# Gated attention block, last stage: GpSimd adds scaled expert outputs in pairs before TensorE sums them

## What is computed

```python
x1 = _layer_norm(x + attn_out, ln1_w, ln1_b)
gates = jax.nn.softmax(x1 @ gate_w.T + gate_b, axis=-1)
_, top_idx = jax.lax.top_k(gates, TOP_K)          # TOP_K = 2 of 8 experts
top_gates = jnp.take_along_axis(gates, top_idx, axis=-1)
expert_outputs = jnp.einsum('bsd,efd->bsef', x1, expert_w) + expert_b[None, None]
sel = jnp.take_along_axis(expert_outputs, top_idx[..., None], axis=2)
moe_out = jnp.sum(sel * top_gates[..., None], axis=2)
return _layer_norm(x1 + moe_out, ln2_w, ln2_b)
```

## Time and profile before

| | us |
|---|---|
| median of 3 runs | 565.8 (564.96 to 565.97) |
| the profiled execution, whole | 566.44 |
| its span, first to last instruction | 564.6 |
| PE busy | 457.0 (81%) |
| DVE busy | 375.2 (66%) |
| POOL busy | 352.3 (62%) |
| ACT busy | 278.5 (49%) |

### The profile page before, as it was taken

One profiled execution on the slowest core, in us unless ns is written; L12 is line 12 of the kernel. 1 busy time (PEld: TensorE's weight loads), 2 busy tenths in 40 slices (PEclk: granted clock), 3 DMA queues, 4 the chain that ended last, 5 costly groups with the idle time before them and its releaser, 6 DMA issues.

```text
span 564.6 us, 16099 instructions
## 1 busy us (share of the span) xinstructions
PE 457.0 (81%) x5728; PEld 281.9 (50%) x5728; DVE 375.2 (66%) x1159; ACT 278.5 (49%) x693; POOL 352.3 (62%) x734
## 2 busy tenths in 40 slices
PE   0247766666667788999999999998969999999993
PEld 0123433333334444666666666664645666666652
DVE  5254665555556757777777777775337899999981
ACT  1114654444444646656566666664644554455431
POOL 3564556553556779988887887851113666766654
PEclk9999977776777869999999999999998999999995
DMA  3344454433444443434344344342000000000000
GB/s 105 94 120 105 105 152 116 110 94 95 110 113 104 103 99 90 98 95 99 96 106 99 96 97 101 95 97 63 9 2 1 10 20 19 20 11 20 20 19 19
DMA packets 96014, 42.72 MB, mean 76 GB/s; under 512 B 19896, under 2 KB 95808, under 8 KB 95936
## 3 DMA queue, kind: packets, MB, share of 16 engines
q1 hardware_dynamic: 86720, 39.60, 27.9%
q10 hardware_dynamic: 9216, 2.10, 1.9%
HBM read 5.75 MB, written 2.10 MB: 14 GB/s over the span
## 4 chain that ended last, share of the span: by engine, by line
SPq 35%; PE 25%; DVE 17%; POOL 12%; issue 6%; DMA 2%; ACT 2%; POOLq 0%; ACTq 0%; DVEq 0%
SPq L192 29%; PE u_bank L426 5%; DVE z_acc L914 4%; PE s_bank L379 3%; PE s_bank L369 3%; POOL xn_all L243 3%; SPq L168 2%; PE u_bank L765 2%; PE s_bank L744 2%; DMA kst<-part 2%; PE st_bank L744 2%; SPq L203 2%; PE u_bank L439 2%; POOL z_rstd_ L642 1%; POOL rstd L233 1%
## 5 line engine op out<-in xcount | busy, mean ns | idle before, releaser
L593 DVE TENSOR_REDUCE nm<-s_bank 128x4 f32<-128x512 f32 x256 | 174.0, 686 | 128.6 <-PE s_bank L379 127.3
L504 ACT ACTIVATE pt<-st_bank 128x512 f32<-128x512 f32 x256 | 150.2, 598 | 144.2 <-PE st_bank L379 105.0
L379 PE MATMUL s_bank<-kst,qst 64*128 64x128 bf16 x1024 | 110.7, 239 | 51.3 <-DMA kst<-part 48.1
L426 PE MATMUL u_bank<-pt,vaug 128*32 128x128 f32 x2048 | 119.2, 309 | 0.1
L379 PEld LDWEIGHTS s_bank<-kst,qst 64*128 64x128 bf16 x1024 | 73.3, 102 | 81.5 <-DMA kst<-part 47.1
L379 PE MATMUL st_bank<-qst,kst 64*128 64x128 bf16 x1024 | 111.2, 235 | 0.0
L379 PEld LDWEIGHTS st_bank<-qst,kst 64*128 64x128 bf16 x1024 | 74.2, 101 | 0.4
L426 PEld LDWEIGHTS u_bank<-pt,vaug 128*32 128x32 f32 x2048 | 42.4, 113 | 31.3 <-issue 8.1
L369 PE MATMUL s_bank<-mqk,esel 64*128 64x256 bf16 x256 | 50.2, 276 | 3.1 <-DMA kst<-part 2.7
L369 PE MATMUL st_bank<-mkq,esel 64*128 64x256 bf16 x256 | 50.2, 276 | 0.0
L285 POOL TENSOR_TENSOR part<-r,part 128x512 bf16<-128x512 f32 x32 | 37.0, 1156 | 2.7
(11 more groups left out here) (118 smaller groups left out, 897.9 us busy)
## 6 DMA issues: line engine op xcount, KB each, us to landing
qst<-part SPq DMA_DIRECT2D x224, 64.0 KB, 2.1
kst<-part SPq DMA_DIRECT2D x224, 64.0 KB, 2.1
x_all<-x SPq DMA_DIRECT2D x16, 128.0 KB, 2.5
c_all<-ctx_in SPq DMA_DIRECT2D x16, 128.0 KB, 2.6
qst<-qrow SPq DMA_DIRECT2D x32, 64.0 KB, 2.1
qst<-mts ACTq DMA_DIRECT2D x64, 32.0 KB, 2.1
out<-z_o SPq DMA_DIRECT2D x16, 128.0 KB, 1.8
ewt<-exp_t SPq DMA_DIRECT2D x1, 512.0 KB
```

The lines of the kernel that those rows point to most:

```text
L379: return pe.matmul(bank[:, j * P:(j + 1) * P], k if keys_first else q, q if keys_first else k, start=not masked, stop=True, skip_group_che ...
L426: ins = pe.matmul(u_bank[b][32 * j:32 * j + 32, r * P:(r + 1) * P], v, pt[m % 4][:, j, :], start=half == 0, stop=half == 1, skip_group_che ...
L504: act.activation(pt[m % 4][:, :, :].rearrange("k j q -> k (j q)"), st_bank[m % 2][:, :], ACT.Exp).then_inc(ex, 1)
L593: dve.tensor_reduce(nm[q % 2][:, first:first + HEADS], s_bank[n % 2][:, :].rearrange("q (j k) -> q j k", j=HEADS), AX_X, ALU.max, negate=T ...
```

## The change

GpSimd adds the four scaled tiles of each sequence two and two (experts 4 and 6, 5 and 7) in one instruction of 128x512 elements, into a new tile `z_gated_pairs`. `gated_sum` then multiplies two tiles by the identity instead of four. A new semaphore `z_yp` stands between them. `gate_experts` now waits for `z_yp` (the pairs of the group before have been added) in place of `z_yb`; the new instruction waits for `z_yg` (ACT has scaled) and, because `z_gated_pairs` is a single buffer, for `z_yb` of the group before. POOL calls the new function last in its step, for group `s - 2`.

```diff
@@ PE, gated_sum
                 pe.wait_ge(z_gtc, g + 1)
-                pe.wait_ge(z_yg, g + 1)
+                pe.wait_ge(z_yp, g + 1)
                 for b in range(G):
                     dst = u_bank[0][:, b * P:(b + 1) * P]
                     pe.matmul(dst, zgt[i][:, b * P:(b + 1) * P], ebs[:, :], start=True, stop=False)
-                    for e in range(HALF):
-                        ins = pe.matmul(dst, idf[:, :], zyg[:, b, e, :], start=False, stop=e == HALF - 1)
+                    for e in range(HALF // 2):
+                        ins = pe.matmul(dst, idf[:, :], zyp[:, b, e, :], start=False, stop=e == HALF // 2 - 1)
                 ins.then_inc(z_yb, 1)
@@ ACT, gate_experts
                 if gc >= 1:
-                    act.wait_ge(z_yb, g)
+                    act.wait_ge(z_yp, g)
@@ POOL
+            def gated_pairs(g, gc):
+                pool.wait_ge(z_yg, g + 1)
+                if gc >= 1:
+                    pool.wait_ge(z_yb, g)
+                pool.tensor_tensor(zyp[:, :, :, :], zyg[:, :, 0:HALF // 2, :], zyg[:, :, HALF // 2:HALF, :],
+                                   ALU.add).then_inc(z_yp, 1)
+
@@ POOL, body
                 if in_z(c, 3):
                     factor2(s - 3, c - 3)
+                if in_z(c, 2):
+                    gated_pairs(s - 2, c - 2)
```

More of the change, by code:

```diff
@@ L659, in gated_block_kernel @@
         zrs2 = sb("z_rstd2_", [P, G]); zy = sb("z_y2", [P, G, P]); zyw = sb("z_yw", [P, G, P])
-        zsum = sb("z_x1_moe", [P, G, P]); zyg = sb("z_gated", [P, G, HALF, P]); zyb = sb("z_ywb", [P, G, P]); zo = two("z_o", [P, G, P])
+        zsum = sb("z_x1_moe", [P, G, P]); zyg = sb("z_gated", [P, G, HALF, P]); zyp = sb("z_gated_pairs", [P, G, HALF // 2, P]); zyb = sb("z_ywb", [P, G, P]); zo = two("z_o", [P, G, P])
         z_at = sem("z_att_copied"); z_ot = sem("z_att_transposed"); z_otc = sem("z_att_t_copied")
@@ L666, in gated_block_kernel @@
         z_gate = sem("z_gate_steps"); z_exp = sem("z_gate_exp"); z_gt = sem("z_gates_transposed")
-        z_gtc = sem("z_gates_t_copied"); z_y = [sem(f"z_experts{k}") for k in range(2)]; z_yg = sem("z_experts_gated"); z_yb = sem("z_expert_bias")
+        z_gtc = sem("z_gates_t_copied"); z_y = [sem(f"z_experts{k}") for k in range(2)]; z_yg = sem("z_experts_gated"); z_yp = sem("z_gated_pairs_summed"); z_yb = sem("z_expert_bias")
         z_acc = sem("z_accumulated"); z_all = sem("z_all_summed_steps"); z_rs2 = sem("z_rstd2_steps"); z_y2s = sem("z_normalised2")
```

## The result

The changed kernel takes 582.78 us (median of 4 runs, 580.06 to 586.02) against 565.38 us for the kernel before. The ratio is 1.0324, with a 95% interval of 1.0251 to 1.0397: slower, as forecast, but 5.2 us beyond the 577.6 us predicted and 0.8 us outside the range. The predicted 577.6 against 565.38 is 1.0216.

The account below looks back on a forecast made before the run. The prediction took DVE's loop, 8.08 us a step, as the bound in the last stage. Its sum was 566.44 + 12.35 - 0.2 - 0.4 = 578.2 us, less 0.6 to the median: 577.6 us, range 565 to 582.

Parts of the forecast that it names:

- The third rival: Last stage: PE was the bound after all, steps of 7.4 us, kernel at 556 us; chance 0.03.
- The relief itself: PE's identity products: four of eight removed a step, freeing 1.2 us a step, costed at nothing in the steady part.
- The mechanism and its place: POOL's addition right behind `z_rstd_` makes the second `z_y` wait until it ends: +0.90 us a step; chance 0.58.
- All rivals for `z_y`: At `z_y`: DVE keeps its turn for both, 570.1 us, chance 0.15; `z_y` shares nothing, 563.8 us, chance 0.17.
- three parts of the 0.90: POOL's addition starts at 0.08 us, is held up to 0.14; second `z_y` ends by 1.53 instead of 0.63.
- 0.03 us in the duration of a power: POOL's `z_rstd_` takes 0.73 us beside `z_n`, 0.70 with DVE idle; read as DVE holding POOL.
- 12.35: Loop term: 14 x 0.90 = 12.6 us for `z_y` of groups 0 to 13, reduced for an existing DVE wait.
- The 0.25 us that DVE waits in the last step before: Last counted `z_y`: DVE waited some 0.25 us anyway, so 12.6 became 12.35 us.
- at its start ... I give it 0.2 us: Start of the steady part, where the chain is still PE's: PE's relief saves 0.2 us.
- -0.4: Drain: PE starts its last sums at about 553.6 instead of 552.25 but saves half of 3.54 us.
- The 0.2% that the prediction takes for the resolution: Measurement: about 0.2%, 1.1 us, can be told from no change.
- The clock rival: Last stage: granted clock falls, PE's 13.6 us a step at half speed bounds, 585 us and more; chance 0.04.

Follow-up runs that it names:

- DVE freed in the kernel before: Kernel before with only `z_two` made by a reduction and `z_others` and `z_top` in PSUM: 569.09 us, ratio 0.9979.
- four sums: Changed kernel with POOL's addition kept but unused, PE summing all four scaled tiles: 582.55 us, ratio 1.0192; second run 585.01 us, 1.0286.
- second profile of the kernel before: The kernel before, unaltered, run again against itself and profiled: 569.50 us, ratio 0.9987.
- two later comparisons: The changed kernel, unaltered, run twice more against the kernel before on other chips: 584.21 us, ratio 1.0262, and 583.30 us, 1.0241.
- PE's relief alone: Kernel before with PE summing only two of four scaled tiles, no POOL addition, experts 6 and 7 left out: 574.07 us, ratio 1.0055.

## Why the prediction was right or wrong

**The bound was read rightly.** The chain named DVE's loop, not PE, and the steps followed DVE's work alone: 9.01 us with PE's work in full or cut. The third rival, PE as the bound, would have given 7.4 us. It was close, though: with DVE freed in the kernel before, PE bounds at 8.00 us. The relief itself was put too high, at 1.2 us a step. For each of the two sequences, four records take 0.66 us where eight took 1.09, so 0.9 us is freed. The steady part of the sum doesn't use this number.

**The mechanism and its place were right, and its price partly by luck.** The addition took 1.263 us (predicted 1.26), began behind `z_rstd_` without a wait, and held one `z_y` of two; the pair took 1.53 instead of 0.60, +0.93 us a step where +0.90 was forecast, steps of 9.01 where 8.98 was. All rivals for `z_y` fell with the 1281 ns. But three parts of the 0.90 were off and nearly cancel: the addition starts 0.03 us before the recorded end of `z_rstd_` and not 0.08 behind it, it isn't held for 0.14 us by the first `z_y`, and the second `z_y` ends 0.34 us behind it and not 0.05: -0.11 - 0.14 + 0.29 = +0.04. That POOL is held by a DVE instruction was read from 0.03 us in the duration of a power, the weakest link; the wide addition shows nothing of it (1.27 us as well where it was moved away from `z_y`).

**The step that failed: the terms for the two ends of the stage.** The forecast came to +11.75 us between the profiles (12.35 - 0.2 - 0.4). It was +17.8:

- *The loop.* 13 steps gave 11.84, and the last step 0.93 more for its `z_y`: 12.8 against the 12.35 forecast. The 0.25 us that DVE waits in the last step before, and that the forecast took off, wasn't saved: with four sums at full clock this step grew by 0.94.
- *The start: "at its start ... I give it 0.2 us".* This term has the wrong sign. In the first step POOL's list now has the first pair addition, which waits for ACT, ahead of `x1`, so `x1` is late and the copy into `z_two` and `z_top` run into it. In the profile after:

```profile
435.97 1.27 POOL L988 TENSOR_TENSOR z_gated_pairs<-z_gated 128x512 f32<-128x512 f32 x1 [0.94 <-ACT z_gated L829]
...
437.19 0.72 POOL L962 TENSOR_TENSOR z_nw<-z_n,l1w 128x256 f32<-128x256 f32 x1
...
437.32 0.63 DVE L890 COPY z_two<-z_sorted 128x4 f32<-128x4 f32 x1
...
438.38 0.38 DVE L897 TENSOR_TENSOR z_top<-z_exps,z_others 128x16 f32<-128x16 f32 x1
```

  0.63 + 0.38 stand where the earlier trace rows had 0.17 + 0.17: +0.67 us. The second run with four sums, whose start was at the clock of the kernel before, has 8.62 us for this step against 7.94, 0.68 more. The prediction says that the new instruction never waits; in the first step it does.

- *The end: "-0.4".* Starting the last sums later was sized rightly: 6.25 us after the last group's first expert addition instead of 4.75, +1.5 against +1.35. But the four groups of products ran at half clock from the start and took 3.67 us rather than the 2.97 that the sum has in it, and the step before them was 0.8 us longer for the same reason. The end gave +1.2 in all. Against the second profile of the kernel before, whose end is 0.7 us shorter, it is +1.9.
- *What differs between executions of one code.* The remaining 3.1 us are 1.25 before the stage and 1.9 in its start and first step. Of these 1.9, two profiles of the kernel before differ by 1.6.

So about half of what is missing in the sum is in its terms, and half lies between executions. How far the result fell outside the range is bad luck in part: by the ratios of the two later comparisons, 1.0262 and 1.0241, a kernel of 565.38 us would come to 580.2 and 579.0 us, inside it. The 0.2% that the prediction takes for the resolution was too little as well; the kernel before against itself has an interval of 0.9956 to 1.0017.

**The clock rival was weighed wrongly.** It had 0.04 and one price, 585 us and more, from PE at half clock through a whole step, which would make it the bound of the 9 us steps. The clock did fall, to 0.90 on average, but for a part of a step at a time (0.81 over a step of 9.01 us), and bounded none of them. It costs where steps are short: 1.28 us in each of three steps with PE's relief alone, and in the last step here. The argument against it, that the clock was 0.9 where PE's busy share was 0.6 to 0.7, holds for three slices of the page and is contradicted by others. From the sixth slice to the thirteenth PE has 6 or 7 tenths too, and the clock has 6 or 7:

```profile
PE   0247766666667788999999999998969999999993
```

The clock's line stands in the earlier trace rows; it also has an 8 in the stage's first whole slice, where the prediction has full speed until the end. A resource that is uncovered by a change needs a price at each place where it bounds, not one for the whole stage. The range ended at 582 because it took the price per step from several rows and the ends from none.

## What to carry to other kernels

When an instruction is added on GpSimd, look at what VectorE has in the same stretch: here, whether it was stretched went by the form and the place of VectorE's operands, and the price went with the length of GpSimd's instruction (0.54 us less for 0.54 us less). Look for pairs that already touch, a small VectorE operation that ends just when a GpSimd one does; moving a VectorE operand to PSUM, or taking a reduction in place of a copy, frees them. Price the first and the last steps of a pipeline by themselves: instructions meet there that don't meet in the middle. Relief for an engine that is full but not the bound gives nothing, and if it is TensorE, it may cost.

## What the runs showed of the hardware

- A copy of four elements a partition on VectorE took 0.17 us alone and 0.65 beside a GpSimd addition; the reduction in its place took 0.16 beside one.
- Of two VectorE instructions that follow each other 0.26 us apart, the first kept its 344 ns beside GpSimd's addition and the second had 1281, in all 15 groups, and ended 0.34 us after the addition. Which engine came first can't be told: the addition is recorded from 0.07 us before the first `z_y`, but also from 0.03 us before the end of the power ahead of it on the same engine.
- Moving one input of `z_y` to PSUM raised it from 0.34 to 0.41 us and took it out of the contention entirely. The Trainium skill's rule on sharing ("SBUF — State Buffer", "Who interferes with whom"), cited before the result, agrees with which instructions stood still here, the 1281 ns of `z_y` above all. That whoever issues first keeps the ports is neither borne out nor refuted, since the order of the two starts is not clear.
- Removing 128 recorded products from TensorE made the kernel 0.55% slower (1.0024 to 1.0087): the granted clock fell in three middle steps, to 0.82 over each 9.35 or 9.36 us, and in the last; before the first of these, TensorE was recorded busy for 7.27 us of 8.09 at full clock.
- The same code met the stage at two different clocks: granted 0.91 or 0.75 from 420 to 440 us in two profiles of the kernel before, and 1.6 us between them.
